# A recurrent network's plain steps: the high half of tanh read ahead of the low-half products, and a new order of the products

## What is computed

```python
def _mlp(y, W1, b1, W2, b2, W3, b3):
    h = jnp.tanh(y @ W1.T + b1)
    h = jnp.tanh(h @ W2.T + b2)
    return h @ W3.T + b3

def _rk4_step(y, dt, params):
    f = lambda z: _mlp(z, *params)
    k1 = f(y)
    k2 = f(y + dt / 2 * k1)
    k3 = f(y + dt / 2 * k2)
    k4 = f(y + dt * k3)
    return y + dt * (k1 + 2 * k2 + 2 * k3 + k4) / 6
...
y0 = x[:, 0]
_, ys = jax.lax.scan(interval, y0, None, length=S - 1)    # x is (16, 256, 128): S = 256, interval = one RK4 step
```

## Time and profile before

| | |
|---|---|
| Median of 3 runs | 2902.06 us (2901.11 to 2902.34) |
| Span of the profiled execution | 2898.5 us |
| TensorE busy | 2815.7 us (97%) |
| VectorE busy | 2353.9 us (81%) |
| ScalarE busy | 1552.0 us (54%) |
| GpSimd busy | 721.4 us (25%) |
| Plain steps lie in the span | from 2156.1 us to its end |

### The profile page before, as it was taken

One profiled execution on the slowest core, in us unless ns is written; L12 is line 12 of the kernel. 1 busy time (PEld: TensorE's weight loads), 2 busy tenths in 40 slices (PEclk: granted clock), 3 DMA queues, 4 the chain that ended last, 5 costly groups with the idle time before them and its releaser, 6 DMA issues.

```text
span 2898.5 us, 207883 instructions
## 1 busy us (share of the span) xinstructions
PE 2815.7 (97%) x81958; PEld 2407.6 (83%) x81958; DVE 2353.9 (81%) x13272; ACT 1552.0 (54%) x10124; POOL 721.4 (25%) x1346
## 2 busy tenths in 40 slices
PE   7789999999999999999999999999999999999999
PEld 3468888888888888888888887888889999999998
DVE  4668888888888888888888887888878888888887
ACT  5446555555555555555555444444445555555555
POOL 5023323323333233233232000111112222222222
PEclk8779999999999999999999999999999999999999
DMA  3000000000000000000000000000000000000000
GB/s 117 0 8 16 11 11 14 11 11 14 11 12 13 11 14 11 11 14 11 11 14 8 1 0 1 0 0 0 0 16 0 0 0 0 0 0 0 0 0 14
DMA packets 21982, 28.21 MB, mean 10 GB/s; under 512 B 4384, under 2 KB 12896, under 8 KB 21544
## 3 DMA queue, kind: packets, MB, share of 16 engines
q1 hardware_dynamic: 21928, 27.48, 3.0%
HBM read 25.24 MB, written 2.23 MB: 9 GB/s over the span
## 4 chain that ended last, share of the span: by engine, by line
PE 92%; DVE 4%; ACT 2%; issue 1%; DMA 0%; SPq 0%; DVEq 0%; ACTq 0%; POOLq 0%; POOL 0%
PE PSUM L678 22%; PE PSUM L684 21%; PE PSUM L885 17%; PE PSUM L739 12%; PE PSUM L669 5%; PE PSUM L881 4%; DVE PSUM L1384 1%; PE PSUM L776 1%; PE PSUM L841 1%; PE PSUM L846 1%; PE PSUM L705 1%; ACT HA L1067 1%; PE PSUM L709 1%; PE PSUM L746 1%; PE PSUM L516 1%
## 5 line engine op out<-in xcount | busy, mean ns | idle before, releaser
L1384 DVE TENSOR_REDUCE PSUM<-PSUM 128x32 f32<-128x64 f32 x2912 | 624.8, 232 | 98.1 <-PE PSUM L684 52.5
L678 PEld LDWEIGHTS PSUM<-HA,RL 128*128 128x128 f16 x11648 | 396.6, 96 | 205.5 <-ACT HA L1067 194.8
L1068 ACT ACTIVATE PSUM<-PSUM 128x32 f32<-128x32 f32 x2912 | 561.3, 194 | 0.0
L1067 ACT ACTIVATE HA<-PSUM 128x32 f16<-128x32 f32 x1456 | 289.1, 199 | 468.1 <-DVE PSUM L1384 468.0
L1067 ACT ACTIVATE HB<-PSUM 128x32 f16<-128x32 f32 x1456 | 289.3, 200 | 466.5 <-DVE PSUM L1384 466.5
L678 PE MATMUL PSUM<-HA,RL 128*128 128x16 f16 x11648 | 512.3, 170 | 15.3 <-ACT HA L1067 7.5
L678 PE MATMUL PSUM<-HB,RLU 128*128 128x16 f16 x11648 | 511.5, 170 | 4.8 <-ACT HB L1067 0.2
L422 POOL TENSOR_TENSOR G<-G 128x512 f16<-128x512 f32 x256 | 296.8, 1159 | 682.8 <-ACT G L1040 682.8
L684 PE MATMUL PSUM<-HA,RH 128*128 128x32 f16 x11648 | 465.4, 177 | 0.0
L684 PE MATMUL PSUM<-HB,RHU 128*128 128x32 f16 x11648 | 464.3, 177 | 0.0
L678 PEld LDWEIGHTS PSUM<-HB,RLU 128*128 128x128 f16 x11648 | 393.9, 96 | 48.1 <-ACT HB L1067 2.4
(11 more groups left out here) (307 smaller groups left out, 6693.1 us busy)
## 6 DMA issues: line engine op xcount, KB each, us to landing
G<-scores SPq DMA_DIRECT2D x64, 256.0 KB, 3.1
N<-in_x SPq DMA_DIRECT2D x8, 256.0 KB, 4.7
NHL<-in_w SPq DMA_DIRECT2D x1, 2048.0 KB, 10.0
STF<-in_w SPq DMA_DIRECT2D x1, 2048.0 KB, 14.5
out<-W2HL SPq DMA_DIRECT2D x8, 256.0 KB, 2.4
G<-in_r SPq DMA_DIRECT2D x1, 1024.0 KB, 5.2
R1K<-in_r SPq DMA_DIRECT2D x1, 256.0 KB, 2.8
R3F<-in_r SPq DMA_DIRECT2D x1, 256.0 KB, 5.4
```

The lines of the kernel that those rows point to most:

```text
L678: mm(out[m // 2][:, 2 * B * (m % 2):2 * B * (m % 2) + B], lo[:, k, m], src[:, k, 0], start=False, stop=False)
L1067: A(hi[:, 2 * h:2 * h + 2, 0], src, ACT.Tanh, scale=1.0 / scale).then_inc(rk_hi, 1)
L1068: A(full, src, ACT.Tanh, scale=1.0 / scale).then_inc(rk_f, 1)
L1384: v.tensor_reduce(bank[:, SUM:SUM + 2 * B].rearrange("p (m b) -> p m b", m=2), bank[:, 0:4 * B].rearrange("p (m c b) -> p m b c", m=2, c=2 ...
```

## The change

SPLIT_ORDER is new. The l products are the last eight; the last L or h product of m0, m1 is h31, the 21st; the last product of m3 is H23, the 31st, and that of m2 is H22, the 32nd. sp_p of group 0 is raised by h31; the new semaphore sp_all is raised by the last l, l00. In front of the first l, l21 (the 33rd), TensorE waits for sp_hi of group 0 of the next layer, that is for the end of the fp16 tanh that reads the sums of m0, m1.

ScalarE's order per layer becomes: fp16 tanh of m0, m1 (after sp_p of group 0, from sums without the l products); fp16 tanh of m2 from the first half of its pair (after sp_p of group 1, ahead of VectorE's sum); fp16 tanh of m3 (after VectorE's sum); then the fp32 tanhs of m0, m1 (after sp_all), of m3 and of m2. The low half remains fp32 tanh minus high half, so it takes up what the high half left out. VectorE sums m3 first, then m2 after ScalarE has read it, and subtracts in the order m0 and m1, m3, m2. Behind the last step ScalarE reads once more, to raise the semaphore that the last layer waits for.

```diff
 SPLIT_ORDER = [(w[0], int(w[1]), int(w[2])) for w in (
-    "L11 L10 h00 L13 L00 h10 h11 h01 L01 L02 L12 h20 L21 L20 l10 l00 H12 l01 L32 h31 L30 h21 l11 l21 L31 H22 l20 "
-    "h30 H02 l30 l31 H32 L22 L03 H23 H33 H03 H13 L23 L33").split()]
+    "h10 L01 h11 L10 L03 L11 L12 h01 h00 L23 L22 h21 L20 L21 h20 L00 L13 L30 L31 h30 h31 L32 L02 L33 H03 H02 H13 H12 "
+    "H33 H32 H23 H22 l21 l01 l31 l20 l10 l30 l11 l00").split()]
...
             def split_layer(s, j, lay, hi, lo, src, opening):
-                waited = set()
+                waited, after_read = set(), False
...
-                    ends = all(SPLIT_OF[m] != SPLIT_OF[b] for _, _, b in SPLIT_ORDER[i + 1:])
+                    if kind == "l" and not after_read:
+                        after_read = True
+                        pe.wait_ge(sp_hi[0], split_count(s, j, lay) + 1)
+                    rest = [(a, b) for a, _, b in SPLIT_ORDER[i + 1:] if SPLIT_OF[b] == SPLIT_OF[m]]
+                    ends = all((a == "l") != (kind == "l") for a, _ in rest)
...
                     if ends:
-                        t.then_inc(sp_p[SPLIT_OF[m]], 1)
+                        t.then_inc(sp_all if kind == "l" else sp_p[SPLIT_OF[m]], 1)
...
-                        for g, ms in enumerate(SPLIT):
-                            act.wait_ge((sp_r if g else sp_p)[g], split_count(s, j, lay))
-                            sl = slice(ms[0], ms[-1] + 1)
-                            A(hi[:, sl, 0], SPLIT_SUM[lay][:, sl], ACT.Tanh, scale=1.0 / scale).then_inc(sp_hi[g], 1)
+                        act.wait_ge(sp_p[0], split_count(s, j, lay))
+                        A(hi[:, 0:2, 0], SPLIT_SUM[lay][:, 0:2], ACT.Tanh, scale=1.0 / scale).then_inc(sp_hi[0], 1)
+                        act.wait_ge(sp_p[1], split_count(s, j, lay))
+                        A(hi[:, 2, 0], PAIRED[lay][0][:, 0:B], ACT.Tanh, scale=1.0 / scale).then_inc(sp_hi[1], 1)
+                        act.wait_ge(sp_r[2], split_count(s, j, lay))
+                        A(hi[:, 3, 0], SPLIT_SUM[lay][:, 3], ACT.Tanh, scale=1.0 / scale).then_inc(sp_hi[2], 1)
+                        for g, done in ((0, sp_all), (2, sp_r[2]), (1, sp_r[1])):
+                            act.wait_ge(done, split_count(s, j, lay))
+                            sl = slice(SPLIT[g][0], SPLIT[g][-1] + 1)
                             A(SPLIT_FULL[lay][:, sl], SPLIT_SUM[lay][:, sl], ACT.Tanh, scale=1.0 / scale).then_inc(sp_f[g], 1)
...
-                            for g in (1, 2):
+                            for g, ready in ((2, sp_p[2]), (1, sp_hi[1])):
                                 ms = SPLIT[g]
-                                dve.wait_ge(sp_p[g], split_count(s, j, lay))
+                                dve.wait_ge(ready, split_count(s, j, lay))
...
-                            for g, ms in enumerate(SPLIT):
+                            for g in (0, 2, 1):
                                 dve.wait_ge(sp_f[g], split_count(s, j, lay))
```

## The result

The changed kernel takes 2960.95 us (median, 2960.24 to 2962.61), with the kernel before beside it at 2901.83: a ratio of 1.0202, interval 1.0188 to 1.0216. It is 2% slower. Forecast were 2943 us in a range of 2918 to 2968, so sign and range hold, and the forecast is 18 us short.

What follows compares the result with a forecast made beforehand. Taken as bound by each layer's TensorE-ScalarE handover. Six layers 7.71, two 2.67, state products 0.20, loop 0.02: 10.60 us a step against 10.04; over 73 steps 41 us more, 2943 us, range 2918 to 2968.

Steps and rivals of the forecast that it cites:

- The hold: TensorE waits in front of l21 for ScalarE's fp16 tanh of m0, m1: 0.46 us from h31, standing 0.185 in every layer; 81%.
- the old handover: In the kernel before, from the last product of m0, m1 through ScalarE's tanh to the first dependent product: 0.46 us.
- The layer: Plain layer from one h31 to the next: 0.46, 0.19, 0.135 and 0.50 us, in all 1.285 against 1.225 before.
- State products, injections, add_low: State products lose cover, +0.20 us a step; two layers with three injections save 0.025 each; add_low stays at 0.15.
- The loop's turn: TensorE's loop turn, right behind the l products: between 0 and 0.15 us a step more, 0.02 taken.
- the loop's own bounds: Range allowed for TensorE's loop turn within the forecast: 0 to +9.5 us on top of 2942.
- the 18 us left for the wait: Range allowed for the wait in front of l21 being 0.03 us shorter or longer: 18 us either way.
- m2, m3 and the low halves: Early m2 tanh covered by 0.28 us, m3 needed later than ready, fp32 tanhs and subtractions covered by 0.035: no effect.
- Low halves in series: fp32 tanhs and VectorE's subtractions do not overlap and set the layer at 1.465 us: 120 us more, 3022; 4%.
- a hold that is covered: l21 let through 0.275 us or less after h31, TensorE never held: layer 1.11, 52 us less, 2850; 7%.
- Even: Wait in front of l21 of 0.38 to 0.40 us, or restart and loop hidden: 2902, within 0.2%; 4%.
- The clock: TensorE's longer standing lowers the granted clock in the plain steps: 93 us more over the whole stage, 3036; 4%.

## Why the prediction was right, and which term was off

*The hold.* Right. 0.465 us from h31 to l21 where 0.46 was taken from the old handover. The choice of that value between 0.265 and 0.64 settled the sign: the release comes with the tanh's end, also where TensorE waits to write and not to read.

*The layer.* Right: 1.287 against 1.285. Its parts are 0.465, 0.32 and 0.495. The change moved the tanh ten products forward, but put the l products, the injections and the state products in line behind it. Moving five products into the cover gave 0.127 a layer back, as this sum says.

*State products, injections, add_low.* Right: 1.387 and 1.3375 against 1.385 and 1.335, and in the hold the state products cost nothing.

*The loop's turn.* Wrong: 0.02 taken, 0.15 as the bound, 0.275 measured, and this is the whole error. The forecast set the turn against the hold: a hold of 0.185 would hide an extra of 0.15. But the turn cannot start in the hold. It starts when the hold ends, and lasts 0.45; only what is queued between the last wait and the turn hides it. The 0.15 in the earlier trace rows was no price of the turn but what eleven products had left of it; with only six left to start, more shows. The upper bound was taken from a place with more cover than the new one, so it was none. Added to the sum, 0.255 x 72 = 18 us make 2961 of 2943. That 2961 lies in the range is partly luck: by the loop's own bounds the top was 2942 + 9.5, and the rest lay in the 18 us left for the wait, which came out as forecast.

*m2, m3 and the low halves.* Nothing was forecast. For m2, tried by itself, that is wrong by about 3 us: its early tanh keeps L23 from waiting in one layer of eight. m3 and the order of the subtractions were not tried. The three fp32 tanhs take 0.34 together after, and VectorE's three subtractions 0.35, where one of them alone takes about 0.18, so both overlap. VectorE in the kernel after, same layer as the handover above:

```profile
2604.95 0.35 DVE L1505 TENSOR_TENSOR HA<-PSUM,HA 128x32 f16<-128x32 f32 x3 [0.16 <-ACT PSUM L1120]
```

These end at 2605.30, and the fp32 tanhs at 2605.08, both ahead of the next first tanh at 2605.37.

*The rivals.* Low halves in series is out with the overlap above, and a hold that is covered with 39.8 us of idle time in front of the high-half weights. "Even" is out by the interval, 1.0188 at the least. The clock is 1.00 from 2300 to 2800 us, though TensorE is held for longer at once than before.

## What to carry to other kernels

A wait put into the middle of a queue makes a loop of what lies from the last product ahead of the read to the wait, and on to the next such product: what can go between read and wait is free up to the length of that handover (0.46 us here), what stands behind the wait is in line, so sort the queue by that first. A stretch of time that hides something must begin after the thing can begin: a loop's turn behind a wait starts when the wait ends, so give it products behind the last wait, or put it where another hold follows. Before steps are put together in one turn, count the instructions of the body.

## What the runs showed of the hardware

- The turn of TensorE's loop takes 0.45 to 0.47 us from its first register operation to the next weight load, 0.21 of it the branch. It starts 0.07 to 0.11 us after the end of the instruction that the last wait ahead of it needs (read in four kernels, with three different waits), and runs beside the products already let go. By the weight loads 0.08 us at most show with sixteen of them still to start, 0.16 with eleven, 0.23 with nine, 0.28 with six.
- A loop body of 1456 instructions on TensorE stays in place; one of 2184 is fetched anew at every turn, 7 us each time and some 170 us over 24 turns, with a granted clock of 0.88 in the stretch.
